# Two cross attentions of a decoder: row scores kept only for their maxima, and a second score product with the keys in rows

## The reference, cut to what matters

```python
# layer 1 (mask); layer 3 is the same with biases and without the mask
q = (x @ Wq).reshape(B, N, HEADS, hd).transpose(0, 2, 1, 3)
k = (context @ Wk).reshape(B, M, HEADS, hd).transpose(0, 2, 1, 3)
v = (context @ Wv).reshape(B, M, HEADS, hd).transpose(0, 2, 1, 3)
scores = jnp.einsum('bhid,bhjd->bhij', q, k) * scale
scores = jnp.where(context_mask[:, None, None, :], scores, max_neg)
attn = jax.nn.softmax(scores, axis=-1)
out = jnp.einsum('bhij,bhjd->bhid', attn, v)
return out @ Wo              # layer 3: relu(out @ W1 + b1) @ W2 + b2
```

## Time and profile before

| | us |
|---|---|
| median of 3 runs (1791.15 to 1797.40) | 1791.43 |
| the profiled execution, first to last instruction (its span) | 1785.6 |
| PE busy, matmuls | 1579.5 (88%) |
| DVE busy | 941.3 (53%) |
| ACT busy | 717.5 (40%) |
| POOL busy | 409.0 (23%) |

### The profile page before, as it was taken

How to read it: one execution, slowest core, us unless ns; L and a number is a source line. 1 busy time by engine, 2 the same in 40 slices (tenths; PEclk the granted TensorE clock), 3 DMA queues, 4 the chain that set the end, 5 groups by cost and what they waited for, 6 DMA issues and landing times.

```text
span 1785.6 us, 40853 instructions
## 1 busy us (share of the span) xinstructions
PE 1579.5 (88%) x14786; PEld 1305.9 (73%) x14786; DVE 941.3 (53%) x2546; ACT 717.5 (40%) x1675; POOL 409.0 (23%) x627
## 2 busy tenths in 40 slices
PE   7998998799987879998797788997988999899998
PEld 6876776678975657776687566775876777689897
DVE  3665877511116657777110562556345667565864
ACT  3334876232323336652222314551755556211110
POOL 2224776500004421112000233432121111000101
PEclk9998999999998999998899798998998999999999
DMA  5343000278951011102686001001001000033232
GB/s 212 147 151 121 28 27 19 106 279 300 321 185 35 1 53 44 29 15 87 254 290 228 13 1 58 28 27 48 1 1 66 23 26 15 24 96 117 81 108 68
DMA packets 41852, 166.72 MB, mean 93 GB/s; under 512 B 5985, under 2 KB 16865, under 8 KB 30177
## 3 DMA queue, kind: packets, MB, share of 16 engines
q1 hardware_dynamic: 39392, 159.14, 25.7%
q0 software_dynamic: 2304, 5.51, 1.0%
HBM read 140.21 MB, written 24.41 MB: 92 GB/s over the span
## 4 chain that ended last, share of the span: by engine, by line
PE 70%; DVE 12%; issue 7%; DMA 3%; POOL 3%; ACT 3%; SPq 1%; DVEq 0%; POOLq 0%; ACTq 0%
PE bank L1688 7%; PE bank L1701 6%; PE bank L1268 6%; PE bank L1630 4%; PE bank L1255 4%; PE bank L1631 4%; PE bank L1632 4%; PE bank L1282 3%; PE bank L795 2%; PE bank L804 2%; PE bank L1238 2%; PE bank L1243 2%; PE bank L896 1%; PE bank L782 1%; DMA xrow<-slots 1%
## 5 line engine op out<-in xcount | busy, mean ns | idle before, releaser
L2053 ACT ACTIVATE arena<-big,nm 112x375 f32<-112x375 f32 x384 | 215.9, 605 | 29.5 <-DVE nm L2894 16.4
L1268 PEld LDWEIGHTS bank<-cst,arena 112*125 112x125 f32 x1152 | 146.6, 192 | 54.0 <-issue 29.0
L1268 PE MATMUL bank<-cst,arena 112*125 112x112 f32 x1152 | 168.0, 283 | 8.8 <-ACT big L2063 5.0
L3150 POOL TENSOR_TENSOR mv<-mv,cst 112x1 f32<-112x1 f32 x88 | 20.1, 228 | 607.3 <-DVE mv L2283 607.3
L2202 ACT ACTIVATE htile<-bank,wup 128x128 f32<-128x128 f32 x280 | 79.7, 368 | 189.7 <-PE bank L1688 189.6
L1688 PE MATMUL bank<-xtile,wup 128*128 128x128 f32 x1120 | 132.8, 278 | 0.3 <-DVE xtile L2997 0.2
L1688 PEld LDWEIGHTS bank<-xtile,wup 128*128 128x128 f32 x1120 | 129.8, 194 | 1.0 <-DVE xtile L2997 0.9
L3013 DVE COPY yrow<-bank 128x256 f32<-128x256 f32 x35 | 14.8, 424 | 217.5 <-PE bank L1701 217.5
L1701 PE MATMUL bank<-wdn,htile 128*128 128x256 f32 x560 | 126.3, 379 | 0.0
L2897 DVE TENSOR_SCALAR_CACHE_REDUCE big<-bank 112x375 f32<-112x375 f32 x192 | 96.0, 543 | 35.3 <-PE bank L1255 33.6
L1701 PEld LDWEIGHTS bank<-wdn,htile 128*128 128x128 f32 x560 | 103.9, 190 | 12.8
(11 more groups left out here) (359 smaller groups left out, 3571.7 us busy)
## 6 DMA issues: line engine op xcount, KB each, us to landing
wup<-in_moe_up SPq DMA_DIRECT2D x35, 1028.0 KB, 7.3
wdn<-in_moe_dn SPq DMA_DIRECT2D x35, 1024.0 KB, 6.1
vspace<-in_ring SPq DMA_DIRECT2D x40, 512.0 KB, 4.2
ctxs<-parts SPq DMA_DIRECT2D x30, 564.0 KB, 3.9
slots<-mlpw SPq DMA_DIRECT2D x11, 1024.0 KB, 6.5
parts<-ctxs SPq DMA_DIRECT2D x8, 564.0 KB, 3.1
xrow<-slots SPq DMA_DIRECT2D x35, 128.0 KB, 5.0
slots<-yrow SPq DMA_DIRECT2D x35, 128.0 KB, 7.0
```

What stands on the lines that cost most here:

```text
L1268: mm = pe.transpose(bank[4 + (3 * g + t) % 2][0:KT, j * T:(j + 1) * T], c_pr[:, g, j, t * KT:(t + 1) * KT], ident[0:T, 0:T])
L2053: nc.scalar.activation(c_pr[:, g, j, :], c_sc[:, g % 2, j, :], ACT.Exp, bias=nm[:, p, h:h + 1], scale=-1.0).then_inc(cexp_done, 1)
```

## The change

It concerns layers 1 and 3, which leave `cross` for new functions `cross_joined`; `cross` is left to layer 0, cut to what that layer needs. Row scores are still computed, but VectorE only takes their minima (with the mask added in layer 1, by a plain reduction in layer 3); no scores and no probabilities are kept in rows. The 16 minima of a row are written into a zeroed tile `j_nm`, turned by four turns (`maxima`) and joined to the negated queries by one pass (`maxima_in`) as a further row of each head's queries; the keys get a row of ones at the same place. For that ScalarE writes each key chunk twice, once for each half of the heads (`keys` with scale and bias, `j_k`). A second score product with the keys in its rows (`scores_t`: per tile of 125 keys four heads by four groups, 16 products of 112 columns, in banks 3 to 6) then gives score minus maximum, and ScalarE's exponential writes the probabilities as the product with the values wants them, 448 columns at a time (`exps`, with the mask as its bias in layer 1). The turns of the probabilities and the copies of turned tiles are gone. `values` is done once per batch. Row scores now use banks 3, 0, 1, 2 in turn, so that bank 3 is shared by row scores and `scores_t`. The output of a batch begins one step later than before, two batches behind; both layers have 8 draining steps; the second key chunk is made in the batch itself, and the first two batches load as before. One small DMA brings the mask in columns at the start of the kernel. The core of the diff (removed lines, unchanged helpers and the GpSimd part are left out; there `spread` moves from g = 1 to g = 3 and the root and the kept rows go to g = 2 and 3):

```diff
@@ tensor engine @@
+    def scores(b, g, p):
+        if g == 0:
+            pe.wait_ge(cqm_ready, at(sub, "c1", b, 1))
+        if g % 2 == 0:
+            pe.wait_ge(ck_done, at(sub, "c2", b, g // 2 + 1))
+        pe.wait_ge(nexp_done, at(sub, "p12", b - 1, 4 * g - 3))
+        for j in range(4):
+            pe.wait_ge(cmax_ready, at(sub, "c16", b, 4 * g + j - 3))
+            if ROW_BANKS[j] == 0 and routed:
+                pe.wait_ge(route_in, 6 + routed)
+            rows = slice(32 * j, 32 * j + 32)
+            pe.matmul(bank[ROW_BANKS[j]][0:T, 0:S2], c_qm[rows, p, g // 2, g % 2, :], j_k[rows, p, g // 2, g % 2, :],
+                      start=True, stop=True).then_inc(cs_ready, 1)
+
+    def maxima(b, more):
+        pe.wait_ge(anm_clear, 3 + sub.index // 10)
+        pe.wait_ge(cmax_ready, at(sub, "c16", b, 16))
+        if more:
+            pe.wait_ge(cq_done, at(sub, "c1", b + 1, 1))
+        pe.wait_ge(xt_done, xt_at(sub, b - 2))
+        for g in range(4):
+            mm = pe.transpose(TL[:, g * T:(g + 1) * T], j_nm[:, g, :], ident[0:T, 0:T])
+        mm.then_inc(anm_ready, 1)
+
+    def scores_t(b, t, p, more):
+        pe.wait_ge(anm_done, at(sub, "n1", b, 1))
+        if more:
+            pe.wait_ge(cmax_ready, at(sub, "c16", b + 1, 4 * t + 1))
+        if t == 0:
+            pe.wait_ge(cv_done, at(sub, "c3", b, 3))
+            pe.wait_ge(cot_in, at(sub, "t1", b, 0))
+        for g in range(4):
+            for i in range(4):
+                if g == 0:
+                    pe.wait_ge(nexp_done, at(sub, "p12", b, 4 * t + i - 3))
+                rows = slice(32 * i, 32 * i + 32)
+                mm = pe.matmul(bank[TURNED_BANKS[i]][0:KT, g * T:(g + 1) * T],
+                               j_k[rows, p, g // 2, g % 2, t * KT:(t + 1) * KT], j_q[rows, g, :], start=True, stop=True)
+                if g == 3:
+                    mm.then_inc(ns_ready, 1)
+
+    def values(b, p):
+        pe.wait_ge(v_zero, 2)
+        pe.wait_ge(nexp_done, at(sub, "p12", b, 12))
+        for g in range(4):
+            for t in range(3):
+                for j in range(4):
+                    h = head_of(g, j)
+                    mm = pe.matmul(OT[32 * j:32 * j + 32, g * T:(g + 1) * T], vbuf[:, p, t, 32 * h:32 * h + 32],
+                                   j_p[:, t, j, g * T:(g + 1) * T], start=(t == 0), stop=(t == 2))
+        mm.then_inc(nv_done, 1)
+
...
+    def step(b, g, p, back, more, one, two):
+
+        if g == 0:
+            if one:
+                maxima(b - 1, back[0])
+            if back[0]:
+                scores(b, g, p)
+                if one:
+                    pe.wait_ge(anm_done, at(sub, "n1", b - 1, 1))
+                value_rows(b, p, 0, TL)
+            if one:
+                idle(b, 2)
+                scores_t(b - 1, 0, 1 - p, back[0])
+            if two:
+                if back[0]:
+                    pe.wait_ge(cv_done, at(sub, "c3", b, 1))
+                elif one:
+                    pe.wait_ge(anm_done, at(sub, "n1", b - 1, 1))
+                else:
+                    pe.wait_ge(xt_done, xt_at(sub, b - 3))
+                output_rows(sub, b - 2)
+        if g == 1:
+            if back[0]:
+                scores(b, g, p)
+                if two:
+                    pe.wait_ge(con_step, at(sub, "t2", b - 1, 0))
+                else:
+                    pe.wait_ge(cv_done, at(sub, "c3", b, 1))
+                keys(b, p, 1, TL)
+            if one:
+                idle(b, 4)
+                scores_t(b - 1, 1, 1 - p, back[0])
+            if two:
+                if back[0]:
+                    pe.wait_ge(ck_done, at(sub, "c2", b, 2))
+                idle(b, 0 if one else 2)
+                output_columns(sub, b - 2)
+        if g == 2:
+            if back[0]:
+                scores(b, g, p)
+            if two:
+                if sub.mlp:
+                    hidden(b - 2)
+                else:
+                    project_rows(sub, b - 2)
+            if one:
+                idle(b, 2)
+                scores_t(b - 1, 2, 1 - p, back[0])
+            if two and sub.mlp:
+                project_hidden(b - 2)
+        if g == 3:
+            if back[0]:
+                scores(b, g, p)
+                if one:
+                    pe.wait_ge(nexp_done, at(sub, "p12", b - 1, 12))
+            if more:
+                keys(b + 1, 1 - p, 0, bank[4])
+            if back[0]:
+                pe.wait_ge(cq_done, at(sub, "c1", b, 1))
+                for t in (1, 2):
+                    value_rows(b, p, t, bank[5][:, (t - 1) * DM:t * DM])
+            if more:
+                if two:
+                    pe.wait_ge(ln_dve, u + 3 * (b - 2) + 1)
+                else:
+                    pe.wait_ge(ck_done, at(sub, "c2", b, 2))
+                q_in(b + 1, 1 - p, TL)
+            if one:
+                idle(b, 4)
+                values(b - 1, 1 - p)
+            if two:
+                if more:
+                    pe.wait_ge(cq_done, at(sub, "c1", b + 1, 1))
+                idle(b, 0 if one else 4)
+                rows_t(sub, b - 2, p)
+        if sub.index == 4 and isinstance(b, int) and b >= B - 2:
+            route(b, g)
+
+    cross_steps(pe, step, 8)
@@ scalar engine @@
+    def keys(b, p, m, src):
+        act.wait_ge(ck_ready, at(sub, "c2", b, m + 1))
+        for e in range(2):
+            ins = nc.scalar.activation(j_k[:, p, m, e, :], src[:, 0:S2], ACT.Identity, scale=w(sub, "keyhalf")[:, e:e + 1],
+                                       bias=w(sub, "keyadd")[:, 2 * m + e:2 * m + e + 1])
+        ins.then_inc(ck_done, 1)
+
...
+    def exps(b, t, p):
+        if t == 0:
+            act.wait_ge(nv_done, at(sub, "v1", b, 0))
+            if sub.mask:
+                act.wait_ge(crow_ready, b + 1)
+        for i in range(4):
+            act.wait_ge(ns_ready, at(sub, "p12", b, 4 * t + i + 1))
+            src = bank[TURNED_BANKS[i]][0:KT, 0:4 * T]
+            if sub.mask:
+                ins = nc.scalar.activation(j_p[:, t, i, :], src, ACT.Exp, bias=mask_add[:, p, t:t + 1])
+            else:
+                ins = nc.scalar.activation(j_p[:, t, i, :], src, ACT.Exp)
+            ins.then_inc(nexp_done, 1)
 
...
+        if g == 0 and back[0]:
+            value_rows(b, p, 0, 1, TL)
+        if g == 1 and back[0]:
+            keys(b, p, 1, TL)
+        if g == 2 and two and sub.mlp:
             hidden(b - 2)
...
+        if g < 3 and one:
+            exps(b - 1, g, 1 - p)
+        if g == 3:
+            if more:
+                keys(b + 1, 1 - p, 0, bank[4])
+            if back[0]:
+                value_rows(b, p, 1, 2, bank[5])
+            if more:
+                q_in(b + 1, 1 - p, TL)
+            if two:
+                rows_in(B + sub.base["row"], b - 2)
         if sub.index == 4 and isinstance(b, int) and (b, g) in ((B - 2, 3), (B, 0)):
             route_exps(1, 0 if b < B else 1)
...
+    cross_steps(act, step, 8)
@@ vector engine @@
+    def row_of(b, p):
+        dve.wait_ge(mask_in[p], 8 * (b - p) + 16 + 16 * (1 - p))
+        dve.tensor_scalar(mask_add[:, p, :], mask_all[:, bass.ds(3 * b, 3)], BIG, -BIG, ALU.mult, ALU.add)
+        dve.tensor_scalar(j_row[:, p, :], maskb[:, p, :], -BIG, BIG, ALU.mult, ALU.add).then_inc(crow_ready, 1)
+
+    def scores_in(b, g, p, js):
+        for j in js:
+            h = 4 * g + j
+            dve.wait_ge(cs_ready, at(sub, "c16", b, h + 1))
+            apart(dve)
+            at_max = j_nm[:, g, 32 * j + 16 - 16 * (g % 2):32 * j + 17 - 16 * (g % 2)]
+            src = bank[ROW_BANKS[j]][0:T, 0:S2]
+            if sub.mask:
+                if h == 0:
+                    dve.wait_ge(crow_ready, b + 1)
+                    apart(dve)
+                dve.wait_ge(cmax_ready, at(sub, "c16", b, h - 1))
+                apart(dve)
+                ins = dve.tensor_tensor_reduce(j_sum[:, j % 2, :], src, j_row[:, p, :], 1.0, -LOWEST,
+                                               ALU.add, ALU.min, at_max)
+            else:
+                ins = dve.tensor_reduce(at_max, src, AX_X, ALU.min)
+            ins.then_inc(cmax_ready, 1)
+
+    def maxima_in(b, p):
+        dve.wait_ge(anm_ready, at(sub, "n1", b, 1))
+        dve.scalar_tensor_tensor(out=j_q.rearrange("p g n -> p (g n)"), in0=c_qm[:, p, :, :, :].rearrange("p m e n -> p (m e n)"),
+                                 scalar=-1.0, in1=TL[:, 0:4 * T], op0=ALU.mult, op1=ALU.add).then_inc(anm_done, 1)
+
...
+    def step(b, g, p, back, more, one, two):
+        if g == 0:
+            if two:
+                output_in(sub, b - 2, nv_done, at(sub, "v1", b - 1, 0))
+            if one:
+                maxima_in(b - 1, 1 - p)
+            if sub.index == 4 and isinstance(b, int) and b == B:
+                route(sub, 7.5)
+            if back[0]:
+                scores_in(b, g, p, range(4))
+        if g == 1:
+            if back[0]:
+                scores_in(b, g, p, (0,))
+            if two:
+                output_normed(sub, b - 2)
```

(31 more changed lines are left out.)

## The result

The changed kernel takes 1825.91 us (median of 4 runs, 1823.64 to 1828.33) against 1794.41 for the kernel before in the same session: ratio 1.0175, 95% interval [1.0154, 1.0196]. It is slower, by 31.5 us; 1793 was forecast, and the measured time lies above the range. The profiled executions have spans of 1826.5 and 1785.6 us, 40.9 apart. That is 9 more than the medians say, by which executions were profiled: a run's time is 1.8 above its span (1828.33 and 1826.5 are the same run), so the profile of before is shorter than all four of its timed runs, while the profile after is the longest of its four.

A forecast was written before the change was run, and what follows sets the result against it. TensorE, busy 88% of the span with nearly no holes, was taken to bound the kernel. Layer 1 +6.9, layer 3 -4.3 and starts -1.4 gave +1.2 us, so 1793 us, with an 8 in 10 range of 1776 to 1808.

The forecast's parts named there:

- What bounds it: Whole kernel: TensorE, busy 88% of the span with nearly no holes in the two stages, sets the time.
- the place of the waits: Middle batch of layer 1: TensorE waits at named places for other engines, 4.4 us a batch.
- the walk: Step-by-step reckoning of one layer 1 batch: 16.4 us work plus 4.4 waits, 20.8; layer 3 22.4; chance 0.50.
- The work of a batch: TensorE's whole queue in a middle batch of layer 1, counted group by group: 16.4 us.
- its balance: TensorE per batch: instructions removed less those added gives 2.4 us less work.
- its list: Prices of each TensorE group in a middle batch of layer 1, together 16.4 us.
- Filling: The two filling batches: held by VectorE's maxima, 16 x 0.47, in both versions, equal within 0.5 us.
- Drain: Batch 7 and the drain: layer 1 46.6 against 43.2 us, +3.4; layer 3 47.0 against 46.8, +0.2.
- Rival 2: Both stages: new holes make TensorE's clock fall, 1.8 us a fall, 1815 if once in each of 13 batches; chance 0.15.
- Layer 2's stage has holes too: Argument against the clock falling at holes in layers 1 and 3; no size given.
- Rival 3: Both stages: hand-overs 0.1 instead of 0.05 us, wider weights 1.1 a tile; +0.8 a batch, 1804; chance 0.11.
- The sum: Whole kernel: layer 1 +6.9, layer 3 -4.3, starts -1.4, together +1.2 us, 1793 us.

The follow-up runs named there:

- e8: The changed kernel with e6's order, plus the last batch's third turned tile right behind the second in both layers' drains; 1789.87 us, ratio 0.9981 to before.
- e6: e4 plus, in layer 1, the next batch's queries between the third turned tile and the row scores of g = 3; 1789.68 us, ratio 0.9973 to before.
- e3: The changed kernel plus products of 0.5 us that nobody reads in TensorE's holes, order unchanged; 1814.82 us, ratio 1.0123 to before.
- e2: The changed kernel with VectorE's output normalisation ahead of the first maximum of g = 1, both layers; 1804.27 us, ratio 1.0069 to before.
- e4: e2 plus batch 0's second key chunk ahead of the row scores, and residual rows turned in the middle of the values; 1794.09 us, ratio 1.001 to before.
- e5: Layer 3 in the new form with e4's order, layer 1 with the cross attention of before; 1784.47 us, ratio 0.994 to before.

## Why the prediction was wrong, by its own steps

- **What bounds it, and the place of the waits: right.** Each hole of the walk is there: before the values rows, before the second key chunk (reckoned 1.5 us, measured 1.08, ended by the multiplication), before the column turns, before the row scores of g = 3 in layer 1 (reckoned 0.8, measured 0.70; absent in layer 3), before the keys of g = 3, before the maxima (0.5 and 0.53). In sum 3.4, reckoned 4.4. The clock of layer 1, 0.87, is under the 0.95 that the prediction had named as a sign of being wrong.
- **The work of a batch: the step that failed first.** Reckoned 16.4, measured 18.95, term by term: row scores 3.28 and 4.76; `scores_t` 2.95 and 3.71; output and rows turned 1.2 and 1.41; keys 1.9 and 2.03; the rest within 0.05 each. The row scores were priced at 0.82 from the earlier trace rows, where nothing waits just ahead of them. Here three groups in four stand behind a wait for the exponential that empties bank 3, and are 1.12 to 1.34 long. In the trace the four products then start 0.05 to 0.27 us apart, where those of the group at 722.12, without a wait, start 0.01, 0.06 and 0.11 apart. VectorE's maxima, which empty the other banks, are out 0.3 us or more before these three groups, so they don't hold them. Likewise `scores_t`: 1.43 where it waits, and from start to next start 1.08 where it doesn't (745.13 to 746.21 in e8), against 0.98 in the earlier trace rows with narrower weights. So a wait costs its hole and then some 0.3 more, and the walk charged the hole alone. What makes the products start apart was not tried; e6 shows only that it goes with the wait. The period was reckoned at 20.8 and 22.4 and was 22.4 and 23.2.
- **The same step could have been caught beforehand.** The prediction held two counts of the work that disagree: 20.2 us a batch less the 2.4 of its balance is 17.8, its list gives 16.4. With 17.8 the walk comes to 22.2, next to the 22.4 measured. Its prices, put on a batch of the kernel before, give 18.8 us where the batch takes 20.1 with hardly a hole. About half of what is missing is one group: in layer 1 the first row scores of a batch took 1.15 to 1.43 before too, from batch 2 on, from start to next start, and the earlier trace rows show two of them, 1.36 and 1.42 long. A third, in a middle batch of before:

```profile
752.13 1.50 PE L1255 MATMUL bank<-big,arena 32*112 32x375 f32 x8
```

- **Filling: failed.** "Equal within 0.5", since VectorE's maxima held both versions. After, TensorE's chain through ScalarE's key writes holds them, at the low clock. 10.2 us more in layer 1, 3.4 in layer 3. Of the layer 1 part, e3 gives back 7.1 and e6 8.1, by a clock that stays up and a shorter chain.
- **Drain: mis-sized.** Reckoned +3.4 and +0.2, measured +11.2 and +3.7. In layer 1, 19.3 us from the first to the last row scores of batch 7 were reckoned at 15.5, and 35.1 behind them at 31.1. The first part holds a hole of 3.3 us before the second key chunk, three times that of the middle batches, and the clock falls towards its end:

```profile
827.14 1.94 PE L1441 MATMUL bank<-ctxs,kv 128*128 128x376 f32 x5 [3.29 <-DVE arena L2526]
```

  VectorE has 3.2 us of the routing (822.2 to 825.4) ahead of the first maximum and the normalisation there; the prediction had put the routing at 0, at most 3. In e2 and e8, with the normalisation first, the hole is still 2.6. In the second part the three rounds of turned tile and exponentials have idle products and batch 6's output between them. e8 took back 4.9 of the 11.2, 2.6 before the last row scores and 2.3 behind; no run moved the routing.
- **The clock.** Rival 2 had a chance of 0.15 and a price of 1.8 us for each fall. In middle batches a fall of some 3.5 us costs 1.4 (23.8 against 22.4), so the price was fair; but the falls were not one in each batch. They lay above all in the filling batches (17 and 7 us long), in batches 6 and 7 (10 each) and in the drain (3). "Layer 2's stage has holes too" was no argument: the largest in its middle batches is 0.53 us, here 1.08 to 1.18. The size of the largest hole doesn't decide it alone: layer 3's middle batches after have one of 1.14 each, with 2.2 us of holes a batch against 3.4 in layer 1, and the clock is 1.00 from its batch 2 to the end of batch 5. The Trainium skill, page "TensorE: Matmul & The Clock Gate", section "A second HAM failure mode: psum-queue depth-cycling", says of another kernel that brief idling between groups of products makes the clock swing between its two levels. By that rule the trace agrees here (0.87 over the stage), and e3 and e4, which shorten the idle times in two ways, agree too.
- **Rival 3, dearer hand-overs.** For the middle batches it is the nearest of the three to what came, and half right: a turned tile takes 1.08 from start to next start, near its 1.1. But the signals are not dearer: TensorE starts 0.06 us after VectorE's multiplication at 728.74. Its 0.8 a batch and 1804 were still too low.
- **The sum.** +1.2 was made of 6.9 - 4.3 - 1.4. Measured: 37.1 + 7.2 - 3.7 + 0.3. Layer 1 misses by 30.2: 10.2 in filling, 12.2 in the five batches, 7.8 in the drain; layer 3 by 11.5: 3.4, 4.6 and 3.5. That the change pays where hidden products cover the waits was right in kind (layer 3's five batches: -4.5 reckoned, +0.1 as written, -10.1 with the new order in e5).

## What to carry to other kernels

When work is moved from VectorE and ScalarE to a TensorE that has no holes, count the new holes before the saved instructions, and price each group that stands behind a wait by rows of groups behind waits. Put the same price list on a batch of the kernel before: if it doesn't give the time that the batch takes, the list is short, as it was here by 1.3 us of 20.1. Look in each engine's list for something that is ready early but written behind something that is not: moving one call on VectorE gave 22 us here. Filling and draining have to be walked like the middle: in layer 1 they are two fifths of the stage, held 21 of the 37 us lost, and all of what e8 still loses there; so the form may pay in one layer and not in the other.

## What the runs showed of the hardware

- Group length behind a wait: 32-row products of 375 columns take 1.12 to 1.34 us for four heads behind a wait for an exponential, and 0.83 to 0.98 without (start to next start); adding independent work ahead of them (e6) gives back both the hole and most of this.
- At the low clock the stage lost 0.3 to 0.4 us for each us spent there (e3: 11.7 for 38; e4 against e6: 2.7 for 6.6; shortest and longest run of e8: 17 for 58), less than the half that it would be if TensorE never waited, since its groups there take up to about twice as long (1.94 and 1.13).
- Adding 67 idle products of 0.5 us, 33 us of TensorE's time, made the kernel 11 us faster (e3).
